# Attention layers: the shifted copies behind the second rotation, and a norm's deviations turned from a column read with stride zero

## What is computed

```
# adapter: x = h + relu(h @ W1[lang] + b1) @ W2[lang] + b2
normed = (x - mean) * rsqrt(var + LN_EPS)             # then gamma, beta

def shift_tokens(t):                                  # second half of the features, one token later
    a, s = jnp.split(t, 2, -1)
    s = jnp.pad(s, ((0, 0), (1, 0), (0, 0)))[:, :-1]
    return jnp.concatenate([a, s], -1)

def attn_layer(x, Wqkv, qs, ksc, Wo):                 # 16 heads of 64
    q, k, v = jnp.split(x @ Wqkv, 3, -1)
    q, k = l2norm(q) * qs, l2norm(k) * ksc
    q = q * cos * scale + rotate_half(q) * sin * scale
    k = k * cos / scale + rotate_half(k) * sin / scale
    return local_attention(q, k, v) @ Wo              # windows of 32, looking one window back

def ffn_layer(x, g, bln, W1, b1, W2, b2):
    xn = (x - mu) / jnp.sqrt(var + 1e-05) * g + bln
    a, gate = jnp.split(xn @ W1 + b1, 2, -1)
    return a * gelu(gate) @ W2 + b2

for i in range(6):
    x = attn_layer(shift_tokens(x), ...) + x
    x = ffn_layer(shift_tokens(x), ...) + x
```

## Time and profile before

| | |
|---|---|
| median of 3 runs | 5840.7 us (5830.07 to 5843.88) |
| the profiled execution | 5848.61 us, its span from first to last instruction 5846.8 us |
| adapter with its norm | about 1550 to 1596 us of the span |
| six layers | 1613 to 5260 us, some 604 us each |
| busy: TensorE, VectorE, ScalarE, GpSimd | 5079.1, 3854.6, 3254.7, 3175.1 us |
| mean granted TensorE clock | 0.937 |

### The profile page before, as it was taken

The page is one execution under the profiler, slowest core; times in us unless marked ns, Lnnn a source line. Parts: engine busy times, 40 slices in busy tenths (PEclk is TensorE's granted clock), DMA queues, the critical chain, the costliest instruction groups (busy, mean ns, idle before and its releaser), DMA issues. The chain is left out here.

```text
span 5846.8 us, 128835 instructions
## 1 busy us (share of the span) xinstructions
PE 5079.1 (87%) x43296; PEld 3299.7 (56%) x43296; DVE 3854.6 (66%) x6824; ACT 3254.7 (56%) x9898; POOL 3175.1 (54%) x1509
## 2 busy tenths in 40 slices
PE   4995899447589999999999999999999899987864
PEld 1331677334357765776577657765777477744542
DVE  2112000554289967997799769986999599956888
ACT  0000000332178866887588858884888488844432
POOL 0000000112389957996699759984999399930018
PEclk9999999759699999999999999999999999998975
DMA  7676555011100000000000000000000000000000
GB/s 208 166 181 143 117 108 109 24 59 50 38 7 0 0 16 5 0 0 16 5 0 0 16 5 0 0 0 20 1 0 0 20 1 0 0 16 14 7 2 14
DMA packets 271956, 199.78 MB, mean 34 GB/s; under 512 B 179032, under 2 KB 254264, under 8 KB 265336
## 3 DMA queue, kind: packets, MB, share of 16 engines
q1 hardware_dynamic: 202073, 119.60, 8.9%
q10 hardware_dynamic: 67487, 71.25, 4.2%
q0 software_dynamic: 2048, 4.20, 0.2%
HBM read 131.83 MB, written 63.16 MB: 33 GB/s over the span
## 5 line engine op out<-in xcount | busy, mean ns | idle before, releaser
L1800 POOL TENSOR_TENSOR rs<-ss,minus_half 128x16 f32<-128x16 f32 x386 | 1127.7, 2921 | 170.9 <-DVE ss L1877 168.8
L1718 ACT ACTIVATE s_ps<-s_ps,low 128x128 f32<-128x128 f32 x3072 | 1064.0, 352 | 1.1 <-DVE low L1888 1.1
L1798 POOL TENSOR_TENSOR t<-t 128x1024 f32<-128x1024 f32 x386 | 911.5, 2361 | 149.4 <-DVE t L1866 149.4
L1805 POOL TENSOR_TENSOR qk<-t,rs 128x1024 f32<-128x1024 f32 x386 | 734.3, 1902 | 60.5 <-POOL rs L1800 23.7
L1718 ACT ACTIVATION_READ_ACCUMULATOR s_ps<-s_ps,low 128x1 f32 x3072 | 673.3, 219 | 0.0
L1888 DVE TENSOR_REDUCE low<-s_ps 128x4 f32<-128x512 f32 x768 | 494.4, 685 | 150.0 <-PE s_ps L1546 150.0
L1897 DVE TENSOR_TENSOR p<-s_ps,rec 128x512 f32<-128x512 f32 x768 | 530.7, 691 | 30.5
L1860 DVE TENSOR_TENSOR t<-qk_ps,rot 128x1024 f32<-128x1024 f32 x386 | 472.4, 1224 | 95.1 <-PE qk_ps L1512 89.5
L1695 ACT ACTIVATE sq<-qk_ps 128x1024 f32<-128x1024 f32 x386 | 395.3, 1024 | 249.1 <-DVE t L1866 249.1
L1732 ACT ACTIVATE pT<-pT_ps 128x512 f32<-128x512 f32 x768 | 457.2, 595 | 104.2 <-PE pT_ps L1552 68.5
L264 PE MATMUL h_ps<-h_x,h_w 9*128 9x512 bf16 x4096 | 441.5, 628 | 84.3 <-DMA h_w<-rows_w1s 63.6
(11 more groups left out here) (404 smaller groups left out, 8781.6 us busy)
## 6 DMA issues: line engine op xcount, KB each, us to landing
h_x<-rows_xs SPq DMA_DIRECT2D x512, 72.0 KB
rows_hs<-h_parts ACTq DMA_DIRECT2D x88, 384.0 KB, 7.1
z_fm<-rows_hs SPq DMA_DIRECT2D x128, 144.0 KB
x_fm<-rows_hs SPq DMA_DIRECT2D x128, 144.0 KB
wqkv<-in_wqkv SPq DMA_DIRECT2D x7, 1536.0 KB, 6.6
o_w<-rows_exs ACTq DMA_DIRECT2D x512, 18.0 KB
rows_xs<-z_fm ACTq DMA_DIRECT2D x12, 384.0 KB, 5.5
rows_exs<-s_exp ACTq DMA_DIRECT2D x9, 512.0 KB, 6.7
```

The costliest lines, as they stand in the source:

```text
L1718: ins = act.activation(s_ps[:, e, i * P:(i + 1) * P], s_ps[:, e, i * P:(i + 1) * P], ACT.Exp, bias=low[:, c % 2, e, i:i + 1], scale=-1.0, ...
L1798: pool.tensor_tensor(t1[:, i, :], t1[:, i, :], t2[:, i, :], ALU.add).then_inc(s_["t12"], 1)
L1800: pool.tensor_tensor(rs[:, i, :], ss[:, i, :], R.minus_half[:, 0:2 * UH], ALU.pow).then_inc(s_["rs"], 1)
L1805: pool.tensor_tensor(qk[:, i, :].rearrange("p (h d) -> p h d", d=DH), t1[:, i, :].rearrange("p (h d) -> p h d", d=DH), rs[:, i, :].unsquee ...
```

## The change

Two edits. VectorE's list of stages has `shift` behind `rotate_swapped` in place of ahead of `rotate`; the call in `tables` stays. And in both norms `diag` and its product on GpSimd are gone: spread takes, for each of the four columns of `rstd`, that column read 128 times over with stride zero, and turns it against the identity into its 128 columns of PSUM, which gives the same numbers. Spread now waits for `rstd`, and the pow that writes `rstd` waits for the spread of the group before.

```
@@ level2_cond, spread on TensorE (the one in level2_layers likewise, with r_ps[j])
-                    pe.wait_ge(s_["diag"], at(k))
+                    pe.wait_ge(s_["rstd"], at(k))
                     pe.wait_ge(s_["xn"], at(k - 1))
-                    pe.matmul(r_ps[:, :], R.ones[:, :], diag[:, :, :].rearrange("p b s -> p (b s)"),
-                              start=True, stop=True).then_inc(s_["spread"], 1)
+                    for b in range(GB):
+                        mm = pe.transpose(r_ps[:, col(b)], rstd[:, b:b + 1].to_broadcast([P, P]), R.ident[:, :])
+                    mm.then_inc(s_["spread"], 1)
@@ level2_layers, rstd_ on GpSimd (the one in level2_cond likewise)
                     pool.wait_ge(s_["f_vare"], at(k))
-                    pool.wait_ge(s_["f_diag"], at(k - 1))
+                    pool.wait_ge(s_["f_spread"], at(k - 1))
                     pool.tensor_tensor(rstd[:, :], var[:, :], R.minus_half[:, 0:GB], ALU.pow).then_inc(s_["f_rstd"], 1)
-                    pool.wait_ge(s_["f_rstd"], at(k))
-                    pool.wait_ge(s_["f_spread"], at(k - 1))
-                    pool.tensor_tensor(diag[:, :, :], R.ident[:, :].unsqueeze(1).to_broadcast([P, GB, P]),
-                                       rstd[:, :].unsqueeze(2).to_broadcast([P, GB, P]), ALU.mult
-                                       ).then_inc(s_["f_diag"], 1)
@@ level2_layers, VectorE
-                    pipeline(dve, NU, 8, [(normalise0, 4), (shift, 0), (rotate, 1), (normalise1, 4), (rotate_swapped, 1), (lows, 3),
+                    pipeline(dve, NU, 8, [(normalise0, 4), (rotate, 1), (normalise1, 4), (rotate_swapped, 1), (shift, 0), (lows, 3),
                                           (sums, 1), (residual, 5)], k0=l * NU,
```

More of the change, by code:

```diff
@@ L1261, in level2_cond @@
         rstd = m.sb("ad_rstd", [P, GB])
-        diag = m.sb("ad_diag", [P, GB, P])
         xn = m.sb("ad_xn", [P, GT])
@@ L1269, in level2_cond @@
         w_ps = [m.ps(f"ad_w_ps{i}", [P, 1024], BF16) for i in range(2)]
-        names = ("hid", "relu", "adapt", "sum", "center", "sq", "var", "var_eps", "rstd", "diag",
+        names = ("hid", "relu", "adapt", "sum", "center", "sq", "var", "var_eps", "rstd",
                  "spread", "xn", "z", "wT", "wTc")
@@ L1366, in rstd_ @@
                     pool.wait_ge(s_["var_eps"], at(k))
-                    pool.wait_ge(s_["diag"], at(k - 1))
+                    pool.wait_ge(s_["spread"], at(k - 1))
                     pool.tensor_tensor(rstd[:, :], var[:, :], R.minus_half[:, 0:GB], ALU.pow).then_inc(s_["rstd"], 1)
-                    pool.wait_ge(s_["rstd"], at(k))
-                    pool.wait_ge(s_["spread"], at(k - 1))
-                    pool.tensor_tensor(diag[:, :, :], R.ident[:, :].unsqueeze(1).to_broadcast([P, GB, P]),
-                                       rstd[:, :].unsqueeze(2).to_broadcast([P, GB, P]), ALU.mult
-                                       ).then_inc(s_["diag"], 1)
                 slots([(rstd_, 2)])
@@ L1458, in level2_layers @@
         rstd = m.sb("ff_rstd", [P, GB])
-        diag = m.sb("ff_diag", [P, GB, P])
         xn = m.sb("ff_xn", [P, GT])
@@ L1473, in level2_layers @@
                  "pTc0", "pTc1", "o", "oTc", "proj", "res",
-                 "f_xs", "f_center", "f_xc", "f_sq", "f_var", "f_vare", "f_rstd", "f_diag", "f_spread", "f_xn",
+                 "f_xs", "f_center", "f_xc", "f_sq", "f_var", "f_vare", "f_rstd", "f_spread", "f_xn",
                  "f_xa", "f_z", "f_gel", "f_h", "f_down", "f_res")
@@ L1608, in spread @@
                     k = l * NG + j
-                    pe.wait_ge(s_["f_diag"], at(k))
+                    pe.wait_ge(s_["f_rstd"], at(k))
                     pe.wait_ge(s_["f_xn"], at(k - 1))
@@ L1614, in spread @@
                         pe.wait_ge(s_["p1"], at(l * NU + NU - 1))
-                    pe.matmul(r_ps[j], R.ones[:, :], diag[:, :, :].rearrange("p b s -> p (b s)"),
-                              start=True, stop=True).then_inc(s_["f_spread"], 1)
+                    for b in range(GB):
+                        mm = pe.transpose(r_ps[j][:, b * P:(b + 1) * P], rstd[:, b:b + 1].to_broadcast([P, P]),
+                                          R.ident[:, :])
+                    mm.then_inc(s_["f_spread"], 1)
                 def feed(l, j, t):
```

2 lines of the change are left out of this document (removed).

## The result

The changed kernel takes 6216.5 us (median of 4 runs, 6211.2 to 6237.9) against 5838.0 for the kernel before beside it (5830.1 to 5843.9): a ratio of **1.0656**, with a 95% interval from 1.0627 to 1.0685. The forecast was 6230 us. The profiled execution has a span of 6209.4 us, 362.6 more than before. Its lines of code are a few numbers lower: add is now L1794, pow L1796, scale L1801, the rotations L1851 and L1857, the copies L1844 and L1845, the minima L1879, the sums L1865, their bound L1868.

A forecast was written before the change was run, and what follows sets the result against it. TensorE was taken as the attention's bound by a hair, GpSimd and VectorE close behind. From the profiled 5848.6 us, +414 for held copies and -25 for turned deviations gave 6237.6, as a median 6230; 8-in-10 range 5860 to 6290.

The forecast's parts named there:

- What bounds the kernel and which edge breaks: Attention: TensorE bounds by a hair; a late VectorE at once delays GpSimd's pow, idle time growing from 0.42 to over 1.4 us.
- The first copy is held until the scale ends plus 0.14 us: Attention units with copies: issued at R+4.51 (R: start of the unit's pow), the first copy waits for GpSimd's scale, to R+5.08.
- The second copy runs behind the add: Same units: GpSimd's add gets in between the copies; the second ends at R+7.45, making the minima 2.40 us late.
- margin of 0.04 us: Between the copies: the add asks at R+5.04, the first copy holds on until R+5.08, so the add gets in.
- The row on who gets in between two copies: Feed-forward trace: a pow beside back-to-back copies took 1.14 us instead of 1.01, read as GpSimd getting in between them.
- A unit with copies takes 10.16 us, one without 7.45: Attention, pow to pow after the change: 17.61 us a pair, +2.23 or +2.47, taken as 2.3; times 180, +414 us.
- A pair before takes 2 x 7.69 = 15.38 us: Attention before the change: one unit is 400/52 = 7.69 us, from 52 pows counted in 400 us.
- TensorE's lateness sets nothing: Attention: the projection starts at R+7.5 instead of R+6.77, 0.8 us late, less than VectorE's 2.4.
- the 86% that was given as a sign: Profile after: TensorE's share in attention was to fall from 99% to about 86%.
- The turned deviations save 25 us: Both norms' spread: four turns take 0.43 us instead of 0.86, saving 21 us in 48 groups and 3.4 in the adapter.
- both copies get in ahead of the add: Rival, attention units with copies: minima only 0.32 us late, +58 less 25, so 5874 us; chance 14%.
- nobody is held: Rival, attention: the copies hide behind the second rotation and nobody is blocked; 5791 to 5816 us, faster; chance 8%.

The follow-up runs named there:

- e9_small_two_input: The changed kernel with the first copy cut in two: 120 columns with one input, then 8 with two; second copy unchanged; ratio 1.0636.
- e8_tensor_copy: The changed kernel with both copies as plain copy instructions, one input each, in the faster mode; 6195.0 us, ratio 1.0607.
- e3_one_input: The changed kernel, same order, each copy a maximum over an axis of length one, so one input; 5757.7 us, ratio 0.9871.
- e7_between: The changed kernel with both two-input copies one place further ahead, right before the second rotation; 6084.3 us, ratio 1.0418.
- e1_turn_only: The changed kernel with the copies back ahead of the first rotation, so only the turned deviations remain; ratio 0.9972.

## Why the prediction was right, step by step

*What bounds the kernel and which edge breaks.* Right: the pow of GpSimd waits for VectorE's bound, and its idle time went from 0.42 us a unit to 68.7/45 = 1.53; over 1.4 was forecast.

*The first copy is held until the scale ends plus 0.14 us.* Right to 0.01 us, 5.09 for 5.08; this rested on five rows of the trace of before. When the copy would issue was wrong and cost nothing: R+4.51 was forecast, the median is R+4.25 (VectorE reaches it sooner), so the copy waits longer for the same end and has 844 ns where 570 followed from the working. The page "SBUF — State Buffer" of the Trainium skill, section "Who interferes with whom", also says that a reduction never takes the shared pair and that copies can take it in their faster mode; the runs with one input and with plain copies agree, 268 ns against 811 in the median. The rule of the Trainium skill that the prediction cites, a block for the whole of a GpSimd instruction that reads SBUF, holds here for the scale and the add and not for the pow: that one reads SBUF too, runs for 2.91 us, and the copies beside it took 274 and 288 ns.

*The second copy runs behind the add.* The outcome was right in the 180 cases that the forecast counted; the other 13 of 193 stand where a layer begins, with no add queued right behind a scale. Its working was not right. The add's request, 0.14 us behind its recorded start, fits the add's own lengthening; that the second copy would get in if the first ended before that request is what `e9_small_two_input` and `e8_tensor_copy` disprove. No margin of 0.04 us decided. The row on who gets in between two copies was the right one to take it from; the arithmetic on top led to the right side by luck, and the 14% for the opposite hung on it.

*A unit with copies takes 10.16 us, one without 7.45.* Measured 10.31 and 7.38, and 10.40 and 7.47 at the loop's return. The 0.15 has two parts: the minima start at R+7.49 in place of R+7.45, and from the minima's start to the sums' start it is 1.32 us and not 1.21 in all 180 units with copies. `e3_one_input` has the 1.32 too; `e7_between`, with the rotation and not the copies right ahead of the minima, has 1.20. So it goes with the copies' place and not with the hold; why stays open.

*A pair before takes 2 x 7.69 = 15.38 us.* Mis-sized: 7.69 came from counting 52 pows in 400 us, and 15.38 happens to be a pair with no loop return in it (7.76 + 7.62). Every fourth pair has 8.31 for 7.76, so the mean is 15.52; after the change the return costs 0.17 us and no longer 0.55. Both errors nearly cancel: (4 x 17.69 + 0.17) / 4 - 15.52 = 2.21 us a pair where 2.3 was taken. The six attention parts grew by 409 us from the third pow to the last, for a forecast of 414. That the total came within 14 us is in part this luck; that the second copy is held and costs over 2 us is not.

*TensorE's lateness sets nothing.* Right: its projection started at 1922.29, R+7.51 for a forecast of R+7.5, and the next unit still ran at 7.38 us, under its old 7.62. TensorE's share fell to 89%, not to the 86% that was given as a sign.

*The turned deviations save 25 us.* `e1_turn_only` has 16, with an interval from 7 to 26. The 0.43 us a group is exact (10.34 to 9.91), and the weights with stride zero cost what others do. The six layers' 48 groups make 21 us of it by that row; the adapter's part is below what the runs can tell.

*The rivals.* That both copies get in ahead of the add does not happen. That nobody is held is what the change would have been with one-input copies: I priced it at 5791 to 5816 us, and `e3_one_input` took 5758. Most of the difference is the loop's return, which my working had averaged away: the attention parts gained 44 us where 25 at most were allowed.

## What to carry to other kernels

Before an instruction of VectorE is moved, ask what GpSimd reads at the new place, and write it with one input and outside the fast copy mode if anything there is long: here 0.56 us of copies took 2.6 us more each time beside a scale and an add, and nothing more as a reduction over an axis of length one. A busy engine in the table may be a held one: compare the duration of the same line in two traces, and look for ends that fall a fixed 0.14 us behind the other engine's. And average a unit's pitch over whole turns of the loop; what is lost only at the return is easy to miss, and here it was over half of what the new place gives once nobody is held (0.6 of 1.0 us in eight units).

## What the runs showed of the hardware

- GpSimd's pow of 16 numbers a partition runs for 2.91 us and held nobody: 181 second copies that started 0.24 to 1.75 us behind its start took 290 ns at most. That GpSimd's reading holds and not its running fits this, but the moment at which the pow reads was not measured.
- What the hold costs is lopsided. The add was lengthened by 0.04 us by a copy that went ahead of it; the copy behind the add was lengthened by 2.06.
- An 8-column instruction that was held ended 0.02 us behind the scale, one of 128 columns 0.14: their own lengths when nobody holds them are 0.15 and 0.27 us. As an estimate from these, the release comes some 0.13 us ahead of GpSimd's recorded end; the second copy (0.29 us long, 0.15 behind the add), the bound (0.17 and 0.03) and the plain copy (0.22 and 0.08) give 0.14.
- An instruction of 16 numbers is held like one of 128: the bound of the sums (two inputs in SBUF) took 0.49 us for 0.17 in a unit without copies of the changed kernel, ending 0.03 us behind the add.
- Four turns from a column read with stride zero start 0.44 us ahead of the next instruction, as four turns of ordinary data do (0.43).
